# Normalising of the tokens on GpSimd, in two operations over all eight tiles of an image

## The reference, cut to what matters

```python
def _ln_t(v, eps=1e-05):
    m = jnp.mean(v, axis=-1, keepdims=True)
    s = jnp.var(v, axis=-1, keepdims=True)
    return (v - m) / jnp.sqrt(s + eps)

# _L1_attn_ref(E, WQ, WK, WV), with E = _ln_t(t)
    Q = jnp.einsum('bsd,ed->bse', E, WQ)
    K = jnp.einsum('bsd,ed->bse', E, WK)
    V = jnp.einsum('bsd,ed->bse', E, WV)
    W = jnp.einsum('bqd,bkd->bqk', Q, K) / scale
    tril = jnp.tril(jnp.ones((S_len, S_len), dtype=W.dtype))
    M = jnp.where(W == 0, jnp.zeros_like(W), tril[None, :, :])
    x_max = jnp.max(W, axis=-1, keepdims=True)
    x_exp = jnp.exp(W - x_max) * M
    A = x_exp / (jnp.sum(x_exp, axis=-1, keepdims=True) + EPS)
    return jnp.einsum('bqk,bkd->bqd', A, V)

# the block
    t = t + _L1_attn_ref(_ln_t(t), L1_attn_WQ, L1_attn_WK, L1_attn_WV)
    t = t + _L1_ffn_ref(_ln_t(t), L1_ffn_router_w, L1_ffn_w1, L1_ffn_w2, L1_ffn_w3)
```

## Time and profile before

| | us |
|---|---|
| median of 3 runs | 2365.29 (2364.75 to 2367.83) |
| the profiled execution | 2363.08 |
| its span, first to last instruction | 2361.3 |

### The profile page before, as it was taken

How to read it: one execution, slowest core, us unless ns; L and a number is a source line. 1 busy time by engine, 2 the same in 40 slices (tenths; PEclk the granted TensorE clock), 3 DMA queues, 4 the chain that set the end, 5 groups by cost and what they waited for, 6 DMA issues and landing times. The chain is left out here.

```text
span 2361.3 us, 46450 instructions
## 1 busy us (share of the span) xinstructions
PE 2031.8 (86%) x11636; PEld 1462.9 (62%) x11637; DVE 1444.6 (61%) x4059; ACT 997.0 (42%) x2116; POOL 1006.0 (43%) x1345
## 2 busy tenths in 40 slices
PE   5999999999999974988888878886099999999998
PEld 4555555555555532655555555554098888888887
DVE  4666666666666642787677777876444444444443
ACT  1455554545555531433333333332044444444443
POOL 2121221212122111145544544555467777777776
PEclk7999999999999996999999999998599999999999
DMA  5222222222222212011111111111134444444443
GB/s 198 61 68 59 69 60 63 66 58 68 57 68 62 63 66 86 19 38 59 46 41 57 44 45 45 53 38 47 55 51 57 56 56 57 57 58 57 56 56 47
DMA packets 175904, 139.58 MB, mean 59 GB/s; under 512 B 33694, under 2 KB 163142, under 8 KB 175558
## 3 DMA queue, kind: packets, MB, share of 16 engines
q0 software_dynamic: 55808, 52.50, 13.9%
q1 hardware_dynamic: 120005, 86.09, 13.1%
HBM read 31.47 MB, written 46.71 MB: 33 GB/s over the span
## 5 line engine op out<-in xcount | busy, mean ns | idle before, releaser
L1457 POOL DMA_INDIRECT out<-f_y,f_rows x272 | 424.1, 1559 | 45.4 <-POOL f_waited L1455 39.8
L395 DVE TENSOR_REDUCE neg_max<-s_bank 128x2 f32<-128x512 f32 x512 | 329.9, 686 | 172.0 <-PE s_bank L600 171.5
L1531 DVE SCALAR_TENSOR_TENSOR f_hidden<-f_silu,f_rows,f_h_bank 128x341 f32<-128x341 f32 x272 | 155.2, 571 | 259.7 <-ACT f_silu L1494 206.9
L489 ACT ACTIVATE probsT<-st_bank 128x512 f32<-128x512 f32 x512 | 277.4, 593 | 36.6 <-PE st_bank L618 35.4
L975 POOL DMA_INDIRECT routed<-a_rows,a_target_idx x256 | 252.2, 985 | 74.5 <-issue 74.5
L1305 PE MATMUL a_score_bank<-a_eT,a_gT 128*128 128x512 f32 x512 | 253.2, 619 | 19.6 <-DVE a_causal_probs L1043 11.0
L630 PE MATMUL o_bank<-probsT,v_ones 128*64 128x512 f32 x1024 | 249.4, 608 | 0.0
L287 POOL TENSOR_TENSOR waited<-nothing 128x1 int32<-128x1 int32 x64 | 12.1, 190 | 547.5 <-DVE q_low L384 547.4
L1582 PE MATMUL f_y_bank<-w,f_hiddenT 114*128 (+1 forms) x1632 | 233.1, 278 | 0.9 <-DVE f_y L1522 0.6
L1494 ACT ACTIVATE f_silu<-f_h_bank 128x341 f32<-128x341 f32 x272 | 124.2, 457 | 211.1 <-PE f_h_bank L1566 164.3
L1582 PEld LDWEIGHTS f_y_bank<-w,f_hiddenT 114*128 114x128 f32 (+1 forms) x1632 | 203.2, 191 | 12.2 <-issue 11.4
(11 more groups left out here) (197 smaller groups left out, 3647.6 us busy)
## 6 DMA issues: line engine op xcount, KB each, us to landing
q_stack<-q_high SPq DMA_DIRECT2D x512, 64.0 KB, 2.4
f_rows<-routed SPq DMA_DIRECT2D x272, 66.0 KB
q_stack<-q_low POOLq DMA_DIRECT2D x256, 64.0 KB, 2.6
a_staged<-X SPq DMA_DIRECT2D x16, 512.0 KB, 3.0
out<-X SPq DMA_DIRECT2D x16, 512.0 KB
X<-in_x SPq DMA_DIRECT2D x1, 6144.0 KB, 22.1
out<-f_y,f_rows POOLq DMA_INDIRECT x272
q_stack<-max_rows SPq DMA_DIRECT2D x256, 4.0 KB
```

The costliest lines, as they stand in the source:

```text
L395: dve.tensor_reduce(neg_max[:, i % 2, CT * j:CT * (j + 1)], s_bank[h % 2][:], AX_X, ALU.max, negate=True).then_inc(max_ready, 1)
L489: act.activation(probsT[:, i % 2, c, lt, :], st_bank[lt][:], ACT.Exp).then_inc(exp_done, 1)
L1457: pool.indirect_dma_start(out=out, out_offset=bass.IndirectOffsetOnAxis(ap=rows[:, i, TOKEN:TOKEN + 1].bitcast(I32), axis=0), in_=y[:, i, ...
```

## The change

`token_norm` moves from VectorE to GpSimd and from step 2 to step 1, directly behind the pow. In place of eight operations of one tile it has two over all eight tiles (1024 elements in each partition): a subtraction of the mean and a multiplication by ln_rs, each with its small operand read again and again by a broadcast. Between the two there is a wait on a new semaphore. Ahead of them stands an operation on one element, `stalled`, which takes the waits for ln_rs and for the previous use of e_tok. Near the start of the stage GpSimd has one more wait.

```diff
             @block.gpsimd
             def _(pool):
                 pool.memset(nothing[:], 0).then_inc(carried, 1)
+                pool.wait_ge(carried, 1)
                 pool.memset(minus_half[:], -0.5).then_inc(consts, 1)
...
+                def token_norm(b):
+                    if not (isinstance(b, int) and b == 0):
+                        pool.wait_ge(shared_full, use_no(b - 2, "e1") + 1)
+                    pool.wait_ge(rs_ready, b + 1)
+
+                    pool.tensor_tensor(stalled[:], nothing[:], nothing[:], ALU.add).then_inc(norm_may_start, 1)
+                    pool.tensor_tensor(e_tok[:], XT[:, b, :, :], ln_mv[:, :, 0:1].to_broadcast([P, TT, P]),
+                                       ALU.subtract).then_inc(e_centred, 1)
+                    pool.wait_ge(e_centred, b + 1)
+                    pool.tensor_tensor(e_tok[:], e_tok[:], ln_rs[:].unsqueeze(2).to_broadcast([P, TT, P]),
+                                       ALU.mult).then_inc(e_ready, 1)
...
                             pool.tensor_tensor(ln_rs[:], ln_ve[:], minus_half[:], ALU.pow).then_inc(rs_ready, 1)
+                            token_norm(b + 1)
...
-                def token_norm(b):
-                    dve.wait_ge(rs_ready, b + 1)
-                    if not (isinstance(b, int) and b == 0):
-                        dve.wait_ge(shared_full, use_no(b - 2, "e1") + 1)
-                    for t in range(TT):
-                        last = dve.tensor_scalar(e_tok[:, t, :], XT[:, b, t, :], ln_mv[:, t, 0:1],
-                                                 ln_rs[:, t:t + 1], ALU.subtract, ALU.mult)
-                    last.then_inc(e_ready, 1)
...
-                        if i == NORM_AT and has(b + 1):
-                            token_norm(b + 1)
```

More of the change, by code:

```diff
@@ L771, in attention_and_routing @@
         waited = sb("waited", [P, 1], I32)
+        stalled = sb("stalled", [P, 1], I32)
         rwT = sb("rwT", [P, EXPERTS])
@@ L845, in attention_and_routing @@
         rs_ready = sem("ln_rs_ready")
+        norm_may_start = sem("norm_may_start")
+        e_centred = sem("e_centred")
         e_ready = sem("e_ready")
```

## The result

The change makes the kernel slower: 2399.47 us (median of 4 runs, 2398.11 to 2406.51) against 2365.02, a ratio of 1.015 (95% interval 1.0128 to 1.0172), or 34.5 us more. The forecast was 46 us more, on the median shown then. The profiled execution is the longest of the four (2406.51 us, span 2404.7).

What follows compares the result with a forecast made beforehand. Bound taken: the order in which engines wait for each other, VectorE's mid-period position leading. Sum 14 x 3.01 + 3.34 = 45.5 us on 2363.08 gives 2408.6; the median, 2.2 above, makes 2411 us; own range 2400 to 2423, chance 0.66.

Steps and rivals of the forecast that it cites:

- Where the change is priced: VectorE's mask of tile 2 waits for GpSimd's diagonal block, queued behind the normalising: 3.01 us later in 14 periods, 3.34 in one.
- the large operation: GpSimd's subtraction and multiplication over 128x1024, between pow and diagonal block 2: 2.30 us each.
- rival A: GpSimd's broadcast operand is free or cheap: 1.72 us per large operation, delay 1.85, time 2393; chance 0.11 with the floor.
- The line through the rows: GpSimd tensor_tensor rows, 193 ns at one element and 455 at 128, give 2.06 ns an element, 2.30 us for 1024.
- The waits between the operations: On GpSimd from pow to diagonal 2: 0.15 us before `stalled`, 0.05 after it, 0.10 between large operations, 0.05 before the diagonal.
- e_tok's lateness covered: e_tok reaches TensorE's transposes 2.4 us later, less than 3.01; tile 4's scores behind them wait for mask 2 anyway.
- The first norm costs nothing: Before the first image, the norm's delay of about 2.5 us hides in TensorE's 17.11 us wait for the staged image.
- The clock: TensorE, idle about 1243 to 1247 each period, falls to half clock at tile 4's scores in most periods; priced at nothing.
- The cover of "about 3 us": Tile 4's row max comes 7.22 us after mask 2 starts; its half-clock scores need 0.6 + 3.6, leaving about 3 us.
- All of it descends from VectorE's position: In mid-period, later row maxes, exponentials, diagonals, masks and TensorE's late sum all follow from where VectorE stands.
- The late sum behind the logits: Late in the period VectorE waits 2.71 us for TensorE's sum, behind logits, ScalarE's rT copies and exponential 5.

Runs made afterwards that it cites:

- e1: The changed kernel again, no edit, on another chip: 2366.44 us against 2335.35 for the kernel before there, ratio 1.0132.
- e2: The changed kernel without the multiplication by ln_rs, so one large GpSimd operation: 2336.05 us, ratio 1.0008 to the kernel before.
- e3: The changed kernel with token_norm behind tile 2's diagonal block on GpSimd, not ahead of it: 2374.53 us, ratio 1.017 to the kernel before.
- e4: The changed kernel with three matmuls nobody reads on TensorE ahead of its wait for e_tok: 2366.36 us, ratio 1.0132 to the kernel before.
- e9: e5 with VectorE's targets one step earlier (TARGETS_AT = 2): 2314.61 us, ratio 0.9911 to the kernel before.
- e7: The kernel before, normalising on VectorE, with TensorE's sum of the values ahead of the shared use: 2304.43 us, ratio 0.9871 to the kernel before.
- e8: The changed kernel with nine unneeded GpSimd operations on scratch data ahead of the first diagonal block: one execution, 2363.70 us.
- e5: e3 with TensorE's sum of the values ahead of the shared use in a step's second place: 2312.03 us, ratio 0.9904 to the kernel before.
- e10: e9 with four matmuls nobody reads on TensorE ahead of its wait for e_tok: 2286.96 us, ratio 0.9794 to the kernel before.

## Why the prediction was right, and where it was not

- **Where the change is priced**: in front of mask 2, not in busy time. Right. From e1 to e2 the distance changes by 1.98 us and the time by 30.4.
- **The term that was mis-sized**: the large operation, 2.30 us forecast, 1.90 measured. It makes 15 x 2 x 0.40 = 12 us, and the forecast with it is 45.5 - 12 = 33.5 for 34.5 measured. That these two agree so well is in part luck: the waits below take another 3 us off, and the 34.5 hold 4.5 us that the sum never had. The measured 2399 us lie just under the forecast's own range (2400 to 2423), and nearer to rival A's 2393 than to 2411. The line through the rows was right for two full operands (2.34). The step that failed is "I take 2.30, because those rows are the same instruction": the broadcast operand was not priced in. Rival A had the reason and took all of the operand's cost away (1.72); the truth lies about two thirds of the way from my value to its (0.40 of 0.58 us). The Trainium skill's figure (GPSIMD Engine Reference, "Performance versus the Vector engine"), halved, gave an estimate of 2.25 us: it agrees with the full operation and not with the broadcast one.
- **The waits between the operations**: 0.15 + 0.05 + 0.10 + 0.05 us forecast. The timeline has 0.14 ahead of `stalled`, and the next start overlaps its end (1263.12 against 1263.16); then 0.08 between the two large ones, and the diagonal block starts at 1266.95, 0.05 before the multiplication's end. In sum 0.2 us a period less than forecast, so the delay is 1.98 and not 3.01 - 0.80 = 2.21.
- **e_tok's lateness covered**: right where the norm stands ahead of diagonal 2 (e1 is 30.4 us over e2, no more than the distance makes). It was a narrow thing: 1 us more and it is the next bound (e3).
- **The first norm costs nothing**: right, 14.09 us of TensorE's wait for the staged image are left.
- **The clock**: it falls at tile 4's scores, as forecast, and there it costs nothing (e4). The cover of "about 3 us" was real: in e9 it is used up and row max 4 waits 1.85 us. The working looked at this place only; falls at tile 6's scores cost about 1.7 us each (e1 and e4), and the kernel before has them too (3.58 us at 1263.47).
- **"All of it descends from VectorE's position"**: right for the delay, which came through in full. The late sum behind the logits was named in the working and read as a link of the chain only; e7 shows that it was 31 us to be had.
- **What stays open**: 34.5 us on the first chip against 30.0 from the distances and 31.1 on the second. In the profiled execution on the first chip the 14 periods grew by 37.0 us, of which 28.1 are the distances (2.32 + 13 x 1.98). Beside the other 9 stand TensorE's waits without a releaser ahead of L1295 (now L1301), which grew by 7.9 us there; over the 14 periods alone it is 13.7 to 20.8 us, and no experiment has any. In the same 14 periods e1 is 23 us shorter than the changed kernel on the first chip. That these waits are the missing part, and much of what makes the first chip slower, fits both numbers and was not tested; what causes them no run shows.

## What to carry to other kernels

Moving work to an idle engine costs whatever stands behind it in that engine's queue: price it by the distance between two instructions of the critical chain, not by busy time. Cutting one wait showed the next four times here (GpSimd's queue, TensorE's order, the shared read, the half clock): the order alone gave 1.3%, a late norm alone cost 1.7%, filler matmuls alone gave nothing, and all of them together, with the targets a step earlier, gave 2.1%. A profile's wait for a sum that stands behind work nobody needs yet is an order to try before any engine is changed.

## What was not expected of the hardware

- GpSimd's tensor_scalar with one operand over 1024 elements took 2.80 us (once, in e8), longer than its tensor_tensor with two (2.34) or with a broadcast one (1.91).
- A VectorE operation over 16 elements took 1.62 us in place of 0.165 beside a GpSimd operation over 1024 (e5 against e7).
- Matmuls that nobody reads, 3.6 us in each period, made a kernel 27.7 us faster (e10 against e9), by keeping the granted clock at 1.00 in place of 0.93.
- On one chip TensorE stood idle for 2.0 us at a time at the same place of most steady periods, with nothing in the profile that released it; the same program on another chip has no such wait (the changed kernel of the result against e1).
